# The routed rows' scatter moved behind the rotary rotation on GpSimd, in a gated attention and mixture-of-experts block

## The reference

```python
q = _rope(proj(_layernorm(x), Wq, bq)); k = _rope(proj(ctx, Wk, bk)); v = proj(ctx, Wv, bv)
scores = einsum('bhqd,bhkd->bhqk', q, k) / sqrt(hd)         # 16 heads, 64 x 64, per batch row
p = softmax(where(mask == 0, NEG_INF, scores))
x = x + tanh(g_xattn) * (einsum('bhqk,bhkd->bhqd', p, v) @ Wo.T + bo)
xf = _layernorm(x); idx = argmax(xf @ Wr + br); gate = softmax(xf @ Wr + br)[idx]
x = x + tanh(g_ffn) * gate * (gelu(xf @ W1[idx] + b1[idx]) @ W2[idx] + b2[idx])
```

## Time and profile before

| what | value |
|---|---|
| median of 3 runs | 287.91 us (287.01 to 290.49) |
| the profiled execution's own time | 287.01 us |
| its span, first to last instruction | 285.2 us |
| mean granted clock of TensorE | 0.958 |
| busy: TensorE, VectorE, ScalarE, GpSimd | 229.3, 189.1, 164.9, 180.3 us |
| scatters L517 | 32, 33.3 us busy, 1041 ns each on the mean |
| rotation L544, L546, L550 | 32 each, 732, 730 and 724 ns |

### The profile page before, as it was taken

The page is one execution under the profiler, slowest core; times in us unless marked ns, Lnnn a source line. Parts: engine busy times, 40 slices in busy tenths (PEclk is TensorE's granted clock), DMA queues, the critical chain, the costliest instruction groups (busy, mean ns, idle before and its releaser), DMA issues.

```text
span 285.2 us, 11006 instructions
## 1 busy us (share of the span) xinstructions
PE 229.3 (80%) x3785; PEld 193.4 (68%) x3785; DVE 189.1 (66%) x639; ACT 164.9 (58%) x482; POOL 180.3 (63%) x222
## 2 busy tenths in 40 slices
PE   1357888987988987789879896598789899999950
PEld 1245677765866765667768675376689799999950
DVE  4546778788798888988867868886575344444310
ACT  1236669696677886568865886436464344444410
POOL 5366757568467889467896686704877654555550
PEclk9999999999799999979996999979999999999995
DMA  7801466546543673314351221333143443110100
GB/s 216 230 15 28 102 148 169 143 103 144 144 129 79 171 177 67 105 32 126 67 150 37 42 48 34 76 85 86 45 143 91 123 119 79 50 33 24 39 21 0
DMA packets 58537, 26.53 MB, mean 93 GB/s; under 512 B 38608, under 2 KB 53989, under 8 KB 58484
## 3 DMA queue, kind: packets, MB, share of 16 engines
q1 hardware_dynamic: 55204, 20.02, 29.3%
q0 software_dynamic: 2272, 4.46, 4.7%
q10 hardware_dynamic: 1008, 1.35, 1.6%
HBM read 16.57 MB, written 5.51 MB: 77 GB/s over the span
## 4 chain that ended last, share of the span: by engine, by line
PE 43%; DVE 19%; issue 11%; ACT 10%; POOL 5%; DMA 5%; SPq 3%; DVEq 0%; POOLq 0%
PE ps L752 13%; DVE mx L1240 5%; PE ps L771 4%; PE ps L795 4%; PE ps L770 3%; PE ps L733 3%; PE ps L735 3%; PE ps L734 3%; ACT vx L644 2%; DVE qk L1185 2%; SPq L411 2%; ACT kT L630 2%; DMA w_r<-in_W_last_row 2%; ACT qk L616 2%; DMA kbd<-kT 2%
## 5 line engine op out<-in xcount | busy, mean ns | idle before, releaser
L565 POOL DMA_INDIRECT out<-fin,got x39 | 37.9, 971 | 28.2 <-DVE fin L1299 23.4
L1240 DVE TENSOR_REDUCE mx<-ps 128x16 f16<-128x1024 f32 x32 | 39.0, 1219 | 12.8 <-PE ps L813 12.7
L752 PE MATMUL ps<-w_f,hT 128*128 x312 | 44.6, 286 | 0.1
L517 POOL DMA_INDIRECT rows<-x_all,dest_i x32 | 33.3, 1041 | 17.0 <-DVE x_all L1075 9.5
L795 PE MATMUL ps<-vx,pr 128*64 128x32 f32 x1024 | 38.0, 229 | 4.9 <-DVE on L1175 4.0
L795 PEld LDWEIGHTS ps<-vx,pr 128*64 128x64 f32 x1024 | 34.5, 144 | 8.9 <-issue 5.3
L544 POOL TENSOR_TENSOR rot<-qk,cf 128x256 f32<-128x256 f32 x32 | 23.4, 732 | 24.7 <-ACT qk L616 17.6
L752 PEld LDWEIGHTS ps<-w_f,hT 128*128 128x128 f32 x312 | 37.8, 191 | 1.1 <-issue 0.3
L1299 DVE SCALAR_TENSOR_TENSOR fin<-ps,got 128x128 f32<-128x128 f32 x39 | 13.7, 351 | 35.9 <-PE ps L752 35.9
L531 POOL TENSOR_TENSOR stk<-rot,stk 128x256 f16<-128x256 f32 x32 | 21.5, 671 | 20.4 <-DVE stk L1253 20.4
L594 ACT ACTIVATE pr<-ps 128x1024 f32<-128x1024 f32 x32 | 32.7, 1021 | 2.2 <-PE ps L843 1.6
(11 more groups left out here) (158 smaller groups left out, 585.1 us busy)
## 6 DMA issues: line engine op xcount, KB each, us to landing
kbd<-kT SPq DMA_DIRECT2D x128, 32.0 KB, 2.5
got<-rows SPq DMA_DIRECT2D x39, 72.0 KB, 2.0
w_f<-in_W_rows SPq DMA_DIRECT2D x8, 256.0 KB, 2.9
w_r<-in_W_last_row SPq DMA_DIRECT2D x8, 256.0 KB, 3.2
w_f<-in_L_ffn_W SPq DMA_DIRECT2D x8, 256.0 KB, 4.7
x_all<-in_x SPq DMA_DIRECT2D x3, 512.0 KB, 5.2
xt_all<-in_x_t SPq DMA_DIRECT2D x3, 512.0 KB, 4.8
ct_all<-in_ctx SPq DMA_DIRECT2D x3, 512.0 KB, 4.5
```

The costliest lines, as they stand in the source:

```text
L517: pool.indirect_dma_start(out=rows, out_offset=bass.IndirectOffsetOnAxis(ap=dest_i[:, t:t + 1], axis=0), in_=x_all[:, t, :], in_offset=Non ...
L565: pool.indirect_dma_start(out=out_d, out_offset=bass.IndirectOffsetOnAxis(ap=got_i[:, u % GOT, R_ID:R_ID + 1], axis=0), in_=fin[:, u % FRI ...
L752: mm = pe.matmul(o, hT[:, par, c, :], w2_f[:, bass.ds(e, 1), c, :].rearrange("p o n -> p (o n)"), start=False, stop=(c == FC - 1))
L1240: dve.tensor_reduce(mx[:, t % 2, :].rearrange("p (w h) -> p w h", w=2)[:, :, 0:8], ps_s[:, :].rearrange("p (w h k) -> p w h k", w=2, k=S), ...
```

## The change

In GpSimd's step the loop over the step's scatters stands behind the three rotation instructions of the new tile, and no longer in front of them. The powers L495 and L503 still come after both. In steps from 32 on there is no tile to rotate, so there the order stays.

```diff
@@ GpSimd, step(i)
                     pool.tensor_tensor(win[:, :, 16:24], f, win[:, :, 8:16], ALU.subtract).then_inc(lo_done, 1)
-                for _ in range(SCATTER_AT.get(i, 0)):
-                    scatter()
                 t = i
                 if live(t):
...
                     pool.tensor_tensor(rot[:, par, :], rot[:, par, :], rot_s[:, par, :], ALU.add).then_inc(rope_done, 1)
+                for _ in range(SCATTER_AT.get(i, 0)):
+                    scatter()
                 if i in RSTD_AT:
                     rstd_of(RSTD_AT[i])
```

## The result

| | before | changed |
|---|---|---|
| median (lowest to highest), 4 runs each on one chip | 287.46 us (285.12 to 290.49) | 293.56 us (292.36 to 295.75) |
| profiled execution: time, span, mean granted clock | 287.01, 285.2, 0.958 | 295.75, 294.0, 0.926 |
| steps 16 to 27, from one projection to the next (traces) | 66.5 us | 72.6 us |

The ratio is 1.0253, with a 95% interval of 1.0188 to 1.0318: slower, though the interval leaves open whether by more than 2%. The median difference is 6.1 us, and in the two profiled executions steps 16 to 27 differ by the same 6.1.

The account below looks back on a forecast made before the run. TensorE led with 43%, its transposes waiting for GpSimd's lo in nearly every step. Lateness 0.65 (15) + 1.0 (23) + 0.3 (25) + 0.4 (28, 29) = +2.35 us: 289.4 profiled, 290.3 us median; range 286.9 to 294.0.

Parts of the forecast that it names:

- the lock for the whole scatter: Rival: VectorE's casts held until the scatter ends, 4.4 us over 11 steps, 294.7 us; sign, casts of 0.5 us; chance 0.07.
- The plain steps: Eleven moved steps without a power instruction behind the rotation: waits for hi cover most; +0.4 us stays, in 28 and 29.
- Step 25: Power instruction L503 behind the rotation: lo at 146.8 against 146.51, +0.3 us.
- Step 23: Power instruction L495 behind the rotation: lo late by 1.2 less a gain of 0.2, +1.0 us.
- a further fall of TensorE's clock: Rival: idle ahead of the transposes in steps 16 and 24 brings low clock; 292.0 or 293.7 us; chance 0.15.
- +0.65: Step 15, power instruction L495 behind the rotation: lo late by 1.2 less a gain of 0.55 us.
- +0.8 "costed at 0": Step 18: lo +0.8 us late, costed at 0 because it lands in step 19, taken as bounded by VectorE.
- the signs, step 24: Sign of being right: transposes' waits for lo grow from 3.3 to about 6 us, step 24 the most lengthened.

Follow-up runs that it names:

- the filled kernel: Changed kernel plus useless matmuls ahead of TensorE's wait for lo in steps 16, 19, 24 and 26, three other waits moved earlier: 288.39 us, ratio 0.9954.
- the extra power: Kernel before, scatters in their old place, one more power instruction behind the rotation in steps 15, 18 and 23: 292.28 us, ratio 1.0133.
- Without L1194: Changed kernel without low weight parts of experts 3 and 4, a maximum over the same numbers replacing L1194 in steps 16 and 19: 295.63 us, ratio 1.0182.
- the runs with five steps moved: Kernel before with the scatter moved behind the rotation only in steps 15, 18, 19, 23 and 25: median 292.04 us, lower group's ratio 1.0025.
- the filling in the kernel before: Kernel before with 24 useless matmuls ahead of the transposes of step 26, three other waits moved earlier: 289.47 us, ratio 0.9998.
- no scatters in 18, 19 and 25: Kernel before, scatters still ahead of the rotation, none in steps 18, 19, 25; two in 20 and 27, one in 21: 288.69 us, ratio 1.0005.

## Why the prediction was right in sign and wrong in size

**Right.** A scatter costs GpSimd 1.2 us of queue (0.15 + 1.01 + 0.02 at 140.50). The rotation of step 23 starts 0.14 behind the end of ScalarE's copy (138.13), as forecast. Beside a scatter the casts take 0.28 to 0.45 us (0.43 at 93.05) against 0.28 undisturbed, and one, at 106.07, takes 0.54. That one passes the 0.5 that was named as the sign of the lock; yet no cast is held for the whole scatter, and the two that start at 170.21 and 170.41, beside the scatter from 170.09 to 171.10, take 0.28 each. So the lock for the whole scatter is out. The plain steps together cost nothing (0.4 forecast). Step 25 was forecast at +0.3: lo ends 2.76 behind the projection of step 26 instead of 2.44, +0.32. Step 23 was forecast at +1.0 and gives +0.67 (1.80 instead of 1.13).

**Wrong, the clock.** The step of the prediction that failed is the one that left a further fall of TensorE's clock out of the sum, as a rival at 0.15 that expected waits of 1.0 to 1.3 us "in steps 16 and 24" and found no fall behind waits as short as those. The waits were 1.66 and 1.92, in steps 16 and 19, longer than the 1.58 behind which the trace before did show a fall. Had they been sized rightly, that same row would have put the fall into the sum. And the ground "no row shows a fall behind a wait as short" held for the rows that were picked: in the same trace the clock falls to 0.50 between 125 and 128 us, behind waits of only 0.53 and 0.79 at the end of step 21. Both executions of the changed kernel with a profile have it behind steps 16, 19 and 26; step 24's 0.94 brought none.

**Wrong, the lateness in 15 and 18.** Forecast were +0.65, and +0.8 "costed at 0". From the projection's start to lo's end, the traces give 1.13 before and 2.52 after in step 16 (+1.39), 1.20 and 2.77 in step 19 (+1.57). Of that, 0.50 and 0.34 are lo itself, running beside L1194. In step 16 some 0.3 more is the scatter of step 15: it costs 1.5 us of queue (0.27 + 1.19 + 0.02), where the prediction took 1.2 for all. I moved lo in time without asking what VectorE does at its new place, though VectorE's order was in the trace. The term put at 0 failed by the clock more than by the slack. Before, the scores of step 19 end at 109.66 and the maximum starts at 110.78: 1.1 us of slack. In the filled kernel lo is as late (+1.53) at full clock, and step 19 takes 6.32, only 0.53 more. In the changed kernel TensorE needs 2.79 us from the transposes to the scores instead of 1.59, and step 19 loses 2.58. Of the signs, step 24 was not the most lengthened: steps 16 and 19 were.

The Trainium skill (SBUF — State Buffer, "SBUF: two separate sides") says that a VectorE instruction with two inputs in SBUF and a GpSimd instruction that reads SBUF shut each other out: the first to start keeps the port pair for its whole length. For lo against L1194 the traces agree within 0.15 us: held until L1194's end, lo would take 1.30 and 1.15 us in the changed kernel and 1.15 with the extra power; measured are 1.16, 1.00 and 1.02. Where L1194 itself starts under a power, it is held for less: 0.94 and 1.05 us, where the rule gives 1.16 and 1.40. For a scatter against the casts of the changed kernel there is no hold for the whole instruction either: 0.26 at most.

**How the 6.1 us split.** Lateness, as the kernels ran: the filled kernel less the kernel before, 68.2 - 66.5 = 1.7 us. With both brought to full clock: before and its filled version give 2.1 us for 10.6 us of low clock, 0.2 each; the filled changed kernel has 2 x 0.03 x 68.2 = 4.1 us of it, so 68.2 - 0.8 - 64.4 = 3.0 us. The forecast 2.35 lies between. The clock has the rest, 3.1 to 4.4 us. The price of 0.2 is a low one: the same step with the same wait, once with the fall and once without, gives 1.05 us in step 26 of the kernel before (7.03 against 5.98, 3.2 us low) and 1.84 in that of the changed one (8.14 against 6.30, 5.0 us low), 0.33 and 0.37 each. That the filled kernel lacks the low stretches, and 4.4 to 4.8 us with them, is shown. The exact split is worked out from single traces.

**Open.** What makes one wait bring the low clock and another not. Over all profiles, in steps 14 to 30, 13 of the 20 unfilled waits of 1.5 us and more ahead of the transposes were followed by a low clock in their step, and none of the 14 of 0.9 to 1.44. Without L1194, waits of 1.82 and 1.90 us were not followed by it and one of 1.08 ahead of the scores was, and the runs with five steps moved fall into two groups. And why two kernels that kept full clock in steps 16 to 27 (the filling in the kernel before, and no scatters in 18, 19 and 25) gained nothing in the end: in their profiles the time is lost ahead of step 16, and in the second behind step 27 too. Step 16 starts between 91.4 and 95.3 us in the eleven profiles, at a mean clock of 0.96 to 0.98 ahead of it, although none but the two filled kernels differs on TensorE there. No run here separates cause from chance in this.

## What to carry to other kernels

Where an engine off the critical path hands TensorE its data, price its delay twice: the wait itself, and the low clock that the trace already shows behind waits of that length, as a likely cost and not a sure one. Compare profiles over the steps that the edit touches, since the steps ahead of them can differ by as much as the effect. Put queue work where the engine waits anyway, as the eleven plain steps show, and not behind a small instruction with no idle time ahead of the hand-over. When an instruction moves in time, look up in the trace what the other engines run in its new place.

## What the runs showed of the hardware

With some 26 matmuls of no use in three of TensorE's waits the clock stood at 2.4 GHz behind them, with the data no earlier: steps 16 to 27 took 68.2 instead of 72.6 us. The same wait can come with and without a fall of the clock: behind 1.90 us step 26 took 8.14 us with it and 6.30 without. An expected gain of 2 us from a full clock in one stretch can vanish over the whole run (ratios 0.9998 and 1.0005). GpSimd's subtraction of 128x256 numbers took 0.66 us undisturbed, and 0.88 to 1.16 where a VectorE instruction with two inputs (L1194) ran beside its start.
